# A fused attention and FP4 feed-forward block: the first step of each unit refilled, the next batch's q and k made earlier, the context scaled and added in one VectorE pass

## Chip, cores and metric

The kernel runs on one core of one Trainium2 chip. The metric is the device time of one launch in microseconds (us). The kernel before takes 4181.91 us, the median of three runs (4179.44 to 4182.91).

## What is computed

The input is x of shape (8, 1024, 512) in float32: 8 batches of 1024 rows.

```
q, k, v = split of (x @ w_qkv) into 3 x 16 heads of 32
scores  = q k^T / sqrt(512)          per head, 1024 x 1024
ctx     = softmax(scores) @ v
x  = layernorm(x + ctx)
g, y = fp4(x) @ fp4(w_gate)^T, fp4(x) @ fp4(w_up)^T       512 -> 1408
x  = layernorm(x + fp4(silu(g) * y) @ fp4(w_down)^T)      1408 -> 512
```

fp4() rounds each block of 16 values to the grid 0, 0.5, 1, 1.5, 2, 3, 4, 6 times the block's own scale.

## The kernel before, in words

After a stage that prepares the weights (some 235 us), a loop runs over the 8 batches. The last quarter of each batch's attention also starts on the next batch: it turns its x and makes its first q and k.

**Attention.** The 16 heads are 4 groups of 4. A unit is one group and one half of the query rows, so a batch has 8 units (`UNITS`), numbered 0 to 7, and a unit has 8 steps (t = 0 to 7), one for each tile of 128 keys. In a step TensorE (PE) makes the scores of 4 heads (`scores`, into the three PSUM banks SC), ScalarE (ACT) takes their exponentials (`exponentials`), and PE multiplies the values by the probabilities of the step before (`weigh`, float32, into the bank CT). GpSimd (POOL) adds up the probabilities of seven of the steps (`sum_probs`).

The softmax needs a row maximum before its exponentials. So 32 further score products per unit are made one unit ahead: PE writes each to a bank of the ring R, and VectorE (DVE) reduces it (`maximum`, jobs `("max", u + 1, n)`). At step 7 PE turns the 16 negated maxima (job `neg`, line 668), DVE splits them into two bf16 parts (`maxima_transposed`, lines 585 and 586), and two DMAs of SyncE (SP) put them below the queries as two more rows (`stack_maxima`, line 521). The first score of the next unit waits for them (`m_loaded`).

**The ring R** has four PSUM banks (`RING = 4`), handed out in the order of the jobs. A job of PE waits in `take` until the job that had its bank before has been read. A projection (`proj`, q, k or v of a group, in four quarters of 0.65 us spread over steps) holds one bank from its first quarter until its low part is made, so the others mostly turn over three banks.

**The end of a unit.** In unit u + 1 PE makes the sums over keys (job `sum`, step 1), turns them (`sumT`, step 2; DVE: `reciprocals`), and turns the context of unit u, four transposes into one bank (`ctx`, step 3, `CTX_STEP`, line 685). DVE's `context_out` multiplies it by the reciprocals in one instruction of 128x512 (line 1282) into `ctx_new`; POOL's `add` (line 1072) then adds `ctx_new` to x.

**Order of work.** `unit_jobs(u, t)` deals the jobs of a step to six places; PE runs a score after places 0, 1, 3 and 4 (`SCORES_AT`) and `weigh` after place 2 (`VALUES_AT`), but in step 0 of a unit it runs `weigh` of the last step first, ahead of place 0. `MADE` says which projection jobs a unit makes and how many quarters in each step. Each engine runs its part of that order in program order. DVE's comes from `vector_steps`: maxima, `neg`, `sumT` and `ctx` in PE's order, a low part behind the next maximum.

**q and k of a group** are copied from `split` to the stacked operands by 12 DMAs for each of k, q0 and q1 (`stack`, line 515), in SP's queue with the loads of x and `stack_maxima`. The first maximum product in unit 7 is the next batch's, and waits for k and q0 of group 4.

**Feed-forward.** Eight tiles of 128 rows, with gate and up products (line 1509), silu, two quantisations on DVE, transposes (lines 1461 and 1471) and the down product (line 1530). In its first tile DVE runs `context_out` of unit 7, `maxima_transposed`, `first_moments(2)` and then the first `quantise_h`, one after another.

## Time and profile before

| | |
|---|---|
| median of 3 runs | 4181.91 us |
| the profiled execution | 4181.16 us, its span 4179.5 us |
| PE busy | 3839.0 us, 92% |
| DVE busy | 3069.8 us, 73% |
| POOL busy | 2279.9 us, 55% |
| ACT busy | 1753.3 us, 42% |
| mean granted TensorE clock | 0.971 of full speed |

The profile is one execution, with all times counted from its start. Between the first and the last batch it repeats every 494 us or so: some 285 us of attention and 210 us of feed-forward. All stretches below are from the fifth batch, which begins near 2203 us, unless a line says otherwise. An engine's busy share does not say whether it waits at the place that matters; the waits and the order of single instructions do. In a timeline a row's duration ends when its result is written, and a next instruction can start before that; the spacing of starts is what a queue of instructions takes.

### The profile page before, as it was taken

Reading aid. Unit: us, or ns where it says so; the run is one execution under the profiler, and the core shown is the slowest. Engines: PE = TensorE matmul, PEld = TensorE weight load, DVE = VectorE, ACT = ScalarE, POOL = GpSimd, SP = SyncE. Lnnn points to the kernel's source line nnn. Section 1 sums busy time; section 2 is a strip of 40 time slices with the busy share of each in tenths; the row PEclk is TensorE's granted clock in tenths of the full one; section 3 lists DMA queues with packets and bytes.
Section 4 is the critical chain, followed back from the end, with each engine's and each line's share of the span. In section 5 each row is a group of like instructions: output and inputs, shape, how many; then the busy total and the mean of one; then the engine's idle time right before and its main releaser. Section 6 shows DMA issues by size and latency. Waiting matters only on the chain. (4 is left out here: it accounts for less than half of the span.)

```text
span 4179.5 us, 61806 instructions
## 1 busy us (share of the span) xinstructions
PE 3839.0 (92%) x22985; PEld 1713.9 (41%) x22985; DVE 3069.8 (73%) x4929; ACT 1753.3 (42%) x3104; POOL 2279.9 (55%) x1446
## 2 busy tenths in 40 slices
PE   3489999999999999999999999999999999999999
PEld 2234344333543345433453335433354334533345
DVE  8866687666866678666786668766686667866777
ACT  3345522554235532455225552255323553245522
POOL 4368622885248832687227862388424873268722
PEclk8689999999999999999999999999999999999999
DMA  5110010111010110111101101101101011010110
GB/s 164 40 59 26 26 49 31 26 31 51 22 34 21 38 43 23 29 31 31 46 18 40 28 21 54 32 21 31 51 23 32 25 34 47 18 36 24 31 49 21
DMA packets 106559, 152.56 MB, mean 37 GB/s; under 512 B 28176, under 2 KB 55568, under 8 KB 106128
## 3 DMA queue, kind: packets, MB, share of 16 engines
q1 hardware_dynamic: 106256, 148.49, 11.5%
q8 instruction: 194, 3.18, 0.3%
q14 instruction: 109, 0.89, 0.1%
HBM read 76.28 MB, written 19.66 MB: 23 GB/s over the span
## 5 line engine op out<-in xcount | busy, mean ns | idle before, releaser
L571 DVE TENSOR_REDUCE mx<-R 128x1 f32<-128x512 f32 x2080 | 1355.6, 686 | 633.4 <-PE R L663 624.0
L1186 ACT ACTIVATE arena<-SC 128x512 f32<-128x512 f32 x1344 | 750.2, 600 | 425.8 <-PE SC L1438 425.6
L1509 PE MATMUL SC<-wgu,split 128*128 128x512 f16 (+1 forms) x3456 | 724.4, 364 | 0.6
L1084 POOL TENSOR_TENSOR wd<-wd,arena 128x1024 f32<-128x1024 f32 x208 | 484.7, 2356 | 39.8 <-ACT arena L1186 39.8
L663 PE MATMUL R<-ks_even,qs_even 96*128 96x512 bf16 x1056 | 418.9, 404 | 88.7 <-issue 44.5
L1110 POOL TENSOR_TENSOR arena<-arena,sc_h 128x704 f32<-128x704 bf16 (+2 forms) x136 | 176.1, 1312 | 576.7 <-DVE arena L496 576.7
L1186 ACT ACTIVATE wd<-SC 128x512 f32<-128x512 f32 x704 | 402.5, 601 | 191.5 <-PE SC L1438 184.7
L1509 PEld LDWEIGHTS SC<-wgu,split 128*128 128x128 f16 x3456 | 338.7, 98 | 344.2 <-issue 13.1
L1227 ACT ACTIVATE arena<-SC,gain 128x512 f32<-128x512 f32 (+1 forms) x192 | 125.1, 651 | 775.1 <-PE R L1509 390.8
L643 PE MATMUL R<-xT,wqkv 128*128 128x512 bf16 x1632 | 433.7, 389 | 4.3 <-issue 4.0
L663 PE MATMUL R<-arena 96*128 96x512 bf16 x1024 | 384.9, 382 | 9.3 <-DVE xT L558 8.1
L1438 PE MATMUL SC<-qs_even,ks_even 98*128 98x512 bf16 x1024 | 367.8, 387 | 4.9 <-ACT arena L1186 4.2
L1438 PE MATMUL SC<-arena 98*128 98x512 bf16 x1024 | 364.5, 385 | 4.7 <-ACT wd L1186 2.1
L663 PEld LDWEIGHTS R<-ks_even,qs_even 96*128 96x128 bf16 x1056 | 106.2, 101 | 374.4 <-DVE mx L571 184.7
L1084 POOL TENSOR_TENSOR spill<-spill,arena 128x1024 f32<-128x1024 f32 x104 | 245.5, 2361 | 6.1 <-ACT arena L1186 5.2
L1084 POOL TENSOR_TENSOR x<-x,arena 128x1024 f32<-128x1024 f32 x104 | 245.1, 2357 | 0.7
L643 PEld LDWEIGHTS R<-xT,wqkv 128*128 128x128 bf16 x1632 | 162.2, 100 | 202.7 <-issue 22.8
L1509 PE MATMUL R<-wgu,split 128*128 128x512 f16 (+1 forms) x1152 | 243.9, 361 | 0.0
L1100 POOL TENSOR_TENSOR split<-spill,sc_x 128x512 f32<-128x512 bf16 x64 | 67.6, 1057 | 319.1 <-DVE spill L496 319.1
L1530 PE MATMUL CT<-wd,arena 128*128 128x512 bf16 x1056 | 234.4, 379 | 0.0
L1530 PE MATMUL R<-wd,arena 128*128 128x512 bf16 x1056 | 234.4, 379 | 0.0
L653 PEld LDWEIGHTS R<-wqkv,xT 128*128 128x128 bf16 x3168 | 200.8, 99 | 58.5 <-issue 10.5
(139 smaller groups left out, 5692.9 us busy)
## 6 DMA issues: line engine op xcount, KB each, us to landing
x<-n_L_attn_embeddings_dram SPq DMA_DIRECT2D x136, 256.0 KB, 2.8
wd<-wd_kept SPq DMA_DIRECT2D x32, 512.0 KB, 5.8
out_dram<-x SPq DMA_DIRECT2D x64, 256.0 KB, 2.0
ks_even<-split SPq DMA_DIRECT2D x204, 64.0 KB, 2.0
qs_even<-split SPq DMA_DIRECT2D x408, 32.0 KB, 1.8
arena<-split SPq DMA_DIRECT2D x192, 64.0 KB, 2.0
arena<-split SPq DMA_DIRECT2D x384, 32.0 KB, 1.8
wd<-wd_kept SPq DMA_DIRECT2D x16, 384.0 KB, 7.5
```

Of the source, the lines that this page charges most:

```text
L571: nc.vector.reduce_max(mx[:, j:j + 1], ring_of(ring, job)[:, :], AX_X).then_inc(max_done, 1)
L643: last = nc.tensor.matmul(ring_of(ring, job)[:, :], wqkv[:, part_w, k, c:c + P], xT[:, part_x, k, half * BANK:(half + 1) * BANK], start=(k ...
L653: last = nc.tensor.matmul(ring_of(ring, job)[:, tt * P:(tt + 1) * P], xT[:, part_x, k, t * P:(t + 1) * P], wqkv[:, part_w, k, c:c + P], st ...
L663: last = nc.tensor.matmul(ring_of(ring, job)[:, :], qs[g % 2][0:STACK, a % 2, hl, t * P:(t + 1) * P], ks[g % 2][0:STACK, hl, half * BANK:( ...
L1084: nc.gpsimd.tensor_tensor(acc[u % 2][i], first, probs_of(s)[:, hs, :], ALU.add).then_inc(pool_sum, 1)
L1100: nc.gpsimd.tensor_tensor(blocks_of(q_x), blocks_of(r_x), spread(sc_x[:, :], H // BLK), ALU.mult).then_inc(qx_done, 1)
L1110: nc.gpsimd.tensor_tensor(blocks_of(q_h[:, cols]), blocks_of(r_h[:, cols]), spread(sc_h[:, c], c.stop - c.start), ALU.mult).then_inc(qh_do ...
L1186: nc.scalar.activation(probs_of(s)[:, hd, :], SC[e % SLOTS][:, :], ACT.Exp, scale=SCALE).then_inc(exp_done, 1)
L1227: nc.scalar.activation(sg[:, k % 2, 0:CHUNKS[c][1]], GU[k % 2][0][:, 0:CHUNKS[c][1]], ACT.Silu, scale=un_gain).then_inc(silu_done, 1)
L1438: nc.tensor.matmul(SC[e % SLOTS][:, :], ks[g % 2][0:STACK_M, hd, t * P:(t + 1) * P], qs[g % 2][0:STACK_M, u % 2, hd, :], start=True, stop= ...
L1509: last = nc.tensor.matmul(GU[kk % 2][which][:, 0:w], xhT[i % 2][:, part_x * KH + k, :], wgu[:, part_w * KH + k, which * I + first:which * ...
L1530: last = nc.tensor.matmul(Y[i % 2], hT[i % 2][:, 2 * TILE_K * c + part_h * tiles + n, :], wd[:, part_w * KI + k, :], start=(k == 0 and m = ...
```

## The change

- **Step 0 of a unit.** Place 0 (two maximum products and a quarter) now runs ahead of `weigh` of the last step, and ScalarE copies the context (`context`) after its own jobs of place 0. Maximum 2 moves to place 1, maximum 4 to place 5. In step 1 the job `sum` runs ahead of a maximum product in its place and no longer behind it.
- **q and k of the next batch.** Job 0 of group 4 moves from unit 6 to unit 5 (four quarters in steps 5, 6 and 7), jobs 1, 2 and 3 are made in unit 6 (two quarters in each of steps 1 to 6), and unit 7 keeps job 4 alone.
- **The context.** `context_out` becomes 16 `scalar_tensor_tensor` instructions of 128x32 (four tiles by four heads). Each reads its part of the ring's bank, multiplies it by one column of `rec` and adds x in place. POOL's `add`, the semaphore `added` and the use of `ctx_new` for it are gone.

```diff
--- before.py
+++ after.py
@@ -89,11 +89,10 @@
 BEFORE_FFN = sum(MAX_STEPS_LAST)
 MADE = (((1, (4, 5)), (1, 1, 1, 1, 1, 1, 1, 1)), ((2, (0, 1)), (1, 1, 1, 1, 1, 1, 1, 1)),
         ((2, (2, 3, 4)), (2, 2, 2, 1, 1, 1, 2, 1)), ((2, (5,)), (3, (0, 1)), (2, 1, 1, 2, 1, 2, 2, 1)),
-        ((3, (2, 3, 4)), (2, 2, 2, 1, 1, 1, 2, 1)), ((3, (5,)), (4, 0, 0, 0, 0, 0, 0, 0)),
-        ((4, (0, 1, 2)), (0, 3, 3, 2, 2, 2, 0, 0)), ((4, (3, 4)), (2, 2, 1, 1, 1, 1, 0, 0)))
+        ((3, (2, 3, 4)), (2, 2, 2, 1, 1, 1, 2, 1)), ((3, (5,)), (4, (0,)), (4, 0, 0, 0, 0, 1, 1, 2)),
+        ((4, (1, 2, 3)), (0, 2, 2, 2, 2, 2, 2, 0)), ((4, (4,)), (1, 1, 0, 1, 1, 0, 0, 0)))
 SCORES_AT, VALUES_AT = (0, 1, 3, 4), 2
 SUM_STEP, SUM_T_STEP, CTX_STEP = 1, 2, 3
-ADD_TILE, ADD_TILE_LAST = 3, 2
 LN_MOMENTS, LN_SCALE = 5, 6
 X_TURNS = [(UNITS - 3, t) for t in range(1, TILES)] + [(UNITS - 2, 0)]
 
@@ -125,7 +124,9 @@
         other += [("xT", X_TURNS.index((u, t)), 0)]
     neg = [("neg", u + 1, 0)] if t == TILES - 1 and not ends else []
     if t == 0:
-        return m[0:1] + q[0:1] + m[1:2], [], m[2:3], m[3:4] + q[1:2], other + m[4:5], q[2:] + m[5:]
+        return m[0:1] + q[0:1] + m[1:2], m[2:3], [], m[3:4] + q[1:2], other, m[4:5] + q[2:] + m[5:]
+    if t == SUM_STEP:
+        return [], m[0:1] + q[0:1], m[1:2], other + m[2:3], m[3:4] + q[1:2], m[4:5] + q[2:] + m[5:]
     return [], m[0:1] + q[0:1], m[1:2], neg + m[2:3] + other, m[3:4] + q[1:2], m[4:5] + q[2:] + m[5:]
 
 
@@ -401,7 +402,6 @@
         wd_saved = sem("wd_saved")
         wd_loaded = [sem(f"wd_loaded{c}") for c in range(len(CHUNKS))]
         ctx_done = sem("ctx_done")
-        added = sem("added")
         chain = sem("chain")
         pool_chain = sem("pool_chain")
         var_done = sem("var_done")
@@ -1065,12 +1065,6 @@
                     nc.gpsimd.memset(ks[1][STACK:STACK_M, :, :], 1.0).then_inc(ones_done, 1)
                     pool.wait_ge(ones_done, 1)
 
-                    def add(u):
-                        pool.wait_ge(ctx_done, u + 1)
-                        rows, g = slice(u % 2 * UNIT_TILES, (u % 2 + 1) * UNIT_TILES), u // 2
-                        xa = x[:, rows, g * P:(g + 1) * P]
-                        nc.gpsimd.tensor_tensor(xa, xa, ctx_new[:, :, :], ALU.add).then_inc(added, 1)
-
                     def sum_probs(u, t, i):
                         s, hs = TILES * u + t, slice(2 * i, 2 * i + 2)
                         pool.wait_ge(exp_done, GROUP * s + 2 * i + 2)
@@ -1116,15 +1110,11 @@
                                 inverse_deviation("x", 0)
                             for i in range(2):
                                 sum_probs(u, t, i)
-                            if t == (ADD_TILE if u < UNITS - 1 else ADD_TILE_LAST) and u >= 1:
-                                add(u - 1)
                     scale_x(0)
                     inverse_deviation("x", 1)
                     for i in range(TILES):
                         if i + 1 < TILES:
                             scale_x(i + 1)
-                        if i == 0:
-                            add(UNITS - 1)
                         if 2 <= i < TILES - 1:
                             inverse_deviation("out", i - 2)
                         if i + 2 < TILES:
@@ -1187,8 +1177,6 @@
                                              scale=SCALE).then_inc(exp_done, 1)
 
                     for s, (u, t) in enumerate(steps):
-                        if t == 0 and u >= 1:
-                            context(u - 1)
                         if (u, t) == (UNITS - 1, LN_SCALE):
                             first_norm(0)
                         for n, place in enumerate(unit_jobs(u, t)):
@@ -1199,6 +1187,8 @@
                                     sums(g)
                                 elif kind == "xT":
                                     x_transposed(g)
+                            if n == 0 and t == 0 and u >= 1:
+                                context(u - 1)
                             if n in SCORES_AT:
                                 exponentials(s, SCORES_AT.index(n))
 
@@ -1274,16 +1264,16 @@
 
                     def context_out(u):
 
-                        job = ("ctx", u, 0)
+                        job, g = ("ctx", u, 0), u // 2
                         dve.wait_ge(ring_full, ring.full(job))
                         dve.wait_ge(rec_done, u + 1)
-                        if u >= 1:
-                            dve.wait_ge(added, u)
-                        nc.vector.tensor_tensor(
-                            ctx_new[:, :, :].rearrange("p t (h d) -> p t h d", h=GROUP),
-                            ring_of(ring, job)[:, :].rearrange("p (t h d) -> p t h d", h=GROUP, d=HD),
-                            rec[:, :, :].unsqueeze(3).to_broadcast([P, UNIT_TILES, GROUP, HD]),
-                            ALU.mult).then_inc(ctx_done, 1)
+                        for i in range(UNIT_TILES):
+                            for hd in range(GROUP):
+                                part = x[:, u % 2 * UNIT_TILES + i, g * P + hd * HD:g * P + (hd + 1) * HD]
+                                last = nc.vector.scalar_tensor_tensor(
+                                    part, ring_of(ring, job)[:, i * P + hd * HD:i * P + (hd + 1) * HD],
+                                    rec[:, i, hd:hd + 1], part, ALU.mult, ALU.add)
+                        last.then_inc(ctx_done, 1)
 
                     def moments(name, i, src, free):
 
@@ -1303,7 +1293,7 @@
 
                     for (u, t), jobs in zip(steps, vector_steps(steps)):
                         if (u, t) == (UNITS - 1, LN_MOMENTS):
-                            dve.wait_ge(added, UNITS - 1)
+                            dve.wait_ge(ctx_done, UNITS - 1)
                             first_moments(0)
                         for kind, a, j in jobs:
                             if kind == "proj3":
@@ -1390,7 +1380,7 @@
                             low_h(i - 1, 2)
                         if i + 2 < TILES:
                             if i == 2:
-                                dve.wait_ge(added, UNITS)
+                                dve.wait_ge(ctx_done, UNITS)
                             first_moments(i + 2)
                         dve.wait_ge(h_done, len(CHUNKS) * (i + 1))
                         quantise_h(i, slice(0, I))
@@ -1483,14 +1473,12 @@
 
                     for s, (u, t) in enumerate(steps):
                         places = unit_jobs(u, t)
-                        if t == 0 and u >= 1:
-                            weigh(s - 1)
                         for n, place in enumerate(places):
                             run(place)
+                            if n == (0 if t == 0 else VALUES_AT) and s > 0:
+                                weigh(s - 1)
                             if n in SCORES_AT:
                                 scores(u, t, SCORES_AT.index(n))
-                            if n == VALUES_AT and t > 0:
-                                weigh(s - 1)
                     weigh(len(steps) - 1)
```

## Rows read from the trace of the kernel before

**Rows 1.** Waits of TensorE from 2200 to 2700 us: us, times, longest.
```profile
PE CT L1451 <- ACT arena L1186: 5.1, 5, 1.2
```

**Rows 2.** Timeline of TensorE at the start of unit 2: start, us, instruction, idle before.
```profile
2269.03 0.28 PE L668 MATMUL R<-identf,neg 128*16 128x128 f32 x1
...
2270.70 1.07 PE L1451 MATMUL CT<-wd,v_even 128*32 128x512 f32 x8 [0.96 <-ACT wd L1186]
...
2272.80 0.59 PE L1438 MATMUL SC<-arena 98*128 98x512 bf16 x2
```

**Rows 3.** SyncE's two DMAs of the maxima there, and their time to landing.
```profile
2270.03 1.14 SPq L521 DMA_DIRECT2D arena<-negT  x2
...
DMA to landing us min/median/max: 1.6/1.7/2.0
```

**Rows 4.** Timeline of TensorE around the context's transposes, units 3 and 4.
```profile
2322.59 0.60 PE L685 MATMUL R<-identf,wd 128*128 128x128 f32 x4
...
2324.77 0.38 PE L663 MATMUL R<-ks_even,qs_even 96*128 96x512 bf16 x1
...
2358.65 0.60 PE L685 MATMUL R<-identf,wd 128*128 128x128 f32 x4
...
2360.20 0.39 PE L663 MATMUL R<-ks_even,qs_even 96*128 96x512 bf16 x1
```

**Rows 5.** Timeline of VectorE around the same context, unit 4.
```profile
2359.46 0.68 DVE L1282 TENSOR_TENSOR ctx_new<-R,rec 128x512 f32<-128x512 f32 x1
2360.05 1.88 DVE L571 TENSOR_REDUCE mx<-R 128x1 f32<-128x512 f32 x3
```

**Rows 6.** VectorE groups by shape: busy us, mean ns.
```profile
L1336 DVE TENSOR_TENSOR arena<-R,arena 128x512 bf16<-128x512 f32 x128 | 85.4, 673 | 0.0
...
L1336 DVE TENSOR_TENSOR arena<-R,arena 128x384 bf16<-128x384 f32 x64 | 35.1, 548 | 10.2 <-ACT arena L1219 10.2
```

**Rows 7.** Timeline of VectorE in the feed-forward stage.
```profile
2549.39 0.74 DVE L1354 SCALAR_TENSOR_TENSOR arena<-R,gain,arena 128x512 f32<-128x512 f32 x1
2550.05 0.68 DVE L1336 TENSOR_TENSOR arena<-R,arena 128x512 bf16<-128x512 f32 x1
...
2552.09 0.18 DVE L1294 BATCH_NORM_AGGREGATE mv<-stats 128x2 f32<-128x6 f32 x1
2552.19 0.66 DVE L1336 TENSOR_TENSOR arena<-R,arena 128x512 bf16<-128x512 f32 x1
```

**Rows 8.** Timeline of TensorE at the start of unit 7.
```profile
2445.55 0.28 PE L668 MATMUL R<-identf,neg 128*16 128x128 f32 x1
...
2451.56 0.38 PE L663 MATMUL R<-ks_even,qs_even 96*128 96x512 bf16 x1 [3.27 <-DMA qs_even<-split]
...
2452.86 1.06 PE L1438 MATMUL SC<-arena 98*128 98x512 bf16 x2
```

**Rows 9.** SyncE's queue in units 6 and 7.
```profile
2433.46 8.50 SPq L515 DMA_DIRECT2D ks_even<-split  x12
2442.65 7.48 SPq L515 DMA_DIRECT2D qs_even<-split  x12
2450.17 1.22 SPq L521 DMA_DIRECT2D arena<-negT  x2
```

**Rows 10.** TensorE at the end of unit 5, then VectorE's last low x.
```profile
2410.81 1.07 PE L1451 MATMUL CT<-arena,v_even 128*32 128x512 f32 x8 [1.23 <-ACT arena L1186]
...
2415.23 0.68 DVE L558 TENSOR_TENSOR xT<-R,xT 128x512 bf16<-128x512 f32 x1
```

**Rows 11.** TensorE at the start of the feed-forward stage.
```profile
2523.59 0.63 PE L1471 MATMUL R<-identf,arena 128*128 128x128 f32 x4 [2.20 <-POOL arena L1110]
2524.05 3.79 PE L1509 MATMUL SC<-wgu,split 128*128 128x384 f16 x12
```

**Rows 12.** That place in two of eight batches: busy by engine, granted clock, DMA.
```profile
2029.50:2035.50 6.00, 4.96 (x32) 3.21 (x32) 5.73 (x11) 1.77 (x3) 2.10 (x2) 1.00 0.17 64
2523.00:2529.00 6.00, 5.41 (x26) 3.18 (x27) 5.69 (x11) 1.19 (x2) 2.10 (x3) 0.72 0.24 92
```

## Prediction

> **What bounds the kernel now.** TensorE is busy for 92% of the span and no other engine for over 73%, so I read its waits first, then the single steps around each edit. The view of its waits names one that comes back at the unit starts: five times a batch (three more stand under the other buffer) PE waits for ScalarE's last exponential [rows 1]. In the timeline this is the 0.96 us of idle time before `weigh`; the next unit's first score then starts at 2272.80, 3.77 us after the transposes of the maxima at 2269.03 [rows 2]. Elsewhere in a unit PE's matmuls start without a gap. So the kernel is bound by PE and the order of its queue, and an edit counts by whether PE stands still for more or less. DVE is close behind it where the context is read: its maxima there run back to back [rows 5].
>
> **Step 0 refilled.** Two maximum products and a quarter, some 1.08 us, now lie in the gap ahead of `weigh`. By itself this would give back the whole gap of about 1.1 us. But the first score also waits for two DMAs of the maxima. They are issued from 2270.03, 1.14 us for both; the second, at about 2270.60, lands 1.7 us later, at 2272.30 [rows 3]. That is 3.27 us after the transposes, and the old first score stood at 3.77 us. With 0.06 us from landing to start it can come at 3.34 us: the gain is 0.43 us, and what was a wait for an exponential becomes a wait for this DMA. Six units (1 to 6) give 2.6 us a batch. In unit 6 extra quarters fill the gap before the transposes too; see below.
>
> **q and k earlier.** In unit 7 PE waits 3.27 us for q0 of the next batch, and its first score comes at 2452.86, 7.31 us after the transposes at 2445.55. The two scores there take 1.06 us where the same two took 0.59 us in unit 2: PE then runs at its lower clock [rows 2, 8]. SP issues q0's 12 DMAs from 2442.65 to 2450.13, and the maxima's two are queued behind them, from 2450.17 [rows 9]. In the new order q0's job ends in step 4 of unit 6 and no longer in step 5, with fewer quarters ahead of it, some 5.4 us earlier (a step there lasts 4.1 to 5.5 us between its first scores in the timeline, and two fewer quarters, 1.3 us, run before it). k's ends a step earlier too and has left the queue by then. So q0's DMAs end near 2444.7, land 1.4 us later, and PE asks for them at 2446.1: just in time. The maxima's DMAs then find the queue free, and the first score comes 3.34 us after the transposes: 7.31 − 3.34 = 3.97 us, and 1.6 us more for eight matmuls of the stretch that no longer take twice their 0.22 us. Together 5.6 us.
>
> The moved quarters are of 0.65 us each (four, 2.6 us, go to unit 5 and leave unit 7). In unit 5, where PE waits 1.23 us before `weigh` and for ScalarE earlier in that step [rows 10], some 1.5 us of them is hidden. In unit 7 three of the four save their time; the fourth, in step 5, covered PE while VectorE and GpSimd normalised the first tile, and saves nothing. In unit 6 step 6 hides 0.25 us. But job 1 now comes first in unit 6, and it needs all eight tiles of x: its first quarter, which started at about 2415.0, must wait for the low part that DVE ends at 2415.91 [rows 10], 0.9 us. Sum: 1.95 − 1.1 + 0.25 − 0.9 = +0.2, taken as +0.3 us.
>
> **The context on VectorE.** This is the part that decides. One instruction that kept DVE for 0.59 us (2359.46 to the next start at 2360.05 [rows 5]) becomes 16, and POOL's add, which PE never waited for, goes. The trace has no 128x32 instruction of this kind. The nearest is the `scalar_tensor_tensor` of the feed-forward stage, with one PSUM source and a per-partition scalar: 0.74 us for 512 columns, 0.66 us from start to start [rows 7]. 128 columns less take 125 ns less (673 to 548 ns, another operation [rows 6]), about 1 ns a column; a slope of 1.04 ns, one column a cycle, fits the two best of these. 480 columns less leave 0.66 − 0.50 = 0.16 us from start to start and 0.25 us for the last one. I take 0.165 us. The lower bound is the shortest spacing in the trace, 0.10 us from a two-column instruction to the next; the upper is 0.25 us, no overlap at all.
>
> A rule bears on this choice. The Trainium skill (VectorE: DVE Perf Modes, "The TRN2 errata") gives a VectorE instruction that reads PSUM 120 cycles plus one per column at 0.96 GHz, and advises tiles of at least 512 elements because many small tiles pay the fixed part each. By it, as an estimate, each would take 158 ns and the forecast would be some 7 us lower. It gives 658 ns for a whole bank, and this trace has 660 ns for the form with a scalar but 590 ns for the plain one [rows 5, 7]; by the plain form's fixed part a small one would cost 0.09 us. The rule and the form with the scalar agree, and they speak against the change.
>
> Who waits? DVE starts the context 0.81 us after PE's transposes at 2358.65 [rows 4, 5]. The bank comes free at 0.81 + 15 × 0.165 + 0.25 = 3.54 us, and PE sees it 0.06 us later: 3.60 us. While a projection holds a bank, the three others go to the context and two maxima, and the third maximum product, the first of step 4, takes the context's bank. It started at 2360.20, 1.55 us after the transposes, and in unit 3, with a quarter between, at 2324.77, 2.18 us after them [rows 4]. So PE stands for 2.05 us in units 2, 4 and 7 and for 1.42 us in units 3 and 6. In unit 1 the next projection takes that bank a matmul later (1.85 us); in unit 5 an x transpose lies between, but its low part waits behind the same 16 (1.9 us). Sum: 6.15 + 2.84 + 3.75 = 12.8 us a batch. DVE has the maxima behind it read again within a step, and PE gets none of it back, since it is what bounds.
>
> The context of unit 7 is read in the first feed-forward tile, ahead of the quantisation for which PE already waits 2.20 us [rows 11]; the next instruction started 0.61 us after it and would now start 16 × 0.165 = 2.64 us after it: 2.0 us more. After that wait the granted clock was 0.72 in the stretch in five of eight batches and 1.00 in three [rows 12]; 12 gate matmuls of 384 columns then took 3.79 us [rows 11], against 12 × 0.17 at the full clock, 1.7 us more. A longer wait should bring the low clock in all eight: 3/8 × 1.7 = 0.6 us. The new waits of 2.05 us lie just under the one that does this, and the idle times of 0.96 and 1.23 us are followed by scores at full pace [rows 2, 10]. I count one such fall a batch: 1.7 us.
>
> **Sum.** Gains 2.6 + 5.6 + 0.3 = 8.5 us; losses 12.8 + 2.0 + 0.6 + 1.7 = 17.1 us; net 8.6 us a batch, 69 us for eight. The profiled execution took 4181.16 us (span 4179.5), 0.75 us under the median of the runs: 4181.2 + 69 = 4250 us. A nanosecond per instruction is worth 7 × 15 + 16 = 121 ns a batch, 0.97 us in all.
>
> **Rivals.**
> - *The small instructions are cheap*, the other side. At 0.10 us each the losses fall by 65 × 0.97 = 63 us and the clock term by up to 14 us: 4173 to 4187 us. It decides at about 0.10 us. For it: the short spacing in the normalisation, and the plain form's small fixed part. Against: the form with a scalar. 13%.
> - *PE does not wait for the context's bank*, since the maxima make room in another way. Then 12.8 and 1.7 go, and 5.9 us are gained: 4134 us. Against it: the product in question starts 0.06 us after the context ends [rows 4, 5]. 10%.
> - *No overlap*: each instruction starts when the one before has ended, 0.25 us. 85 × 0.97 = 82 us more: 4332 us. The Trainium skill (same page, "Two Vector instructions with no wait between them") holds an instruction back only where its operands start in other quadrants than the last one's; here all start at partition 0, which speaks against it, and no row shows it. 10%.
> - *The low clock after nearly every context wait*: six falls and not one, 5 × 1.7 = 8.5 us a batch: 4318 us. For it: the wait of 2.20 us does so in five of eight. The Trainium skill (TensorE: Matmul & The Clock Gate, "The HAM clock gate") has activity hold the clock up, so each standstill counts against it. 12%.
> - *q and k do not come early enough*: a DMA or DVE step is late and half of the 5.6 us or all of it stays: 4272 to 4295 us. 10%.
>
> My own case has 45%, and its own range is 4215 to 4285 us. The range to 8 in 10 leaves out the second rival and the far end of the third: 4165 to 4320 us. What a measurement here can tell from no change is 0.2%, 8.4 us. Faster than that holds the second rival and most of the first, 0.20; within it 0.08; slower 0.72.
>
> **What would show it.** Right: 16 instructions on the context's line about 0.165 us apart; PE waits of 1.4 to 2.1 us on it in step 4 of every unit but the first; first scores 3.3 us after the transposes, released by the DMA of the maxima; no wait for q0 in unit 7; a feed-forward wait of about 4.2 us. Wrong: a spacing near 0.10 us, PE waits under 1 us there, or a low clock in most units.

## The result, and the profile after

The changed kernel takes 4255.58 us (median of four runs, 4252.03 to 4264.54) against 4181.99 us for the kernel before on the same chip: a ratio of 1.018, 95% interval 1.0163 to 1.0198. It is slower by 74 us. The profiled execution is the slowest of the four, 4264.54 us with a span of 4262.9 us, so its rows add up to some 9 us more than the median. All stretches are again of the fifth batch, which now lies near 2243 to 2750 us, unless the text says otherwise.

The page's first part and the waits of TensorE over the whole span (us, times, longest):

```profile
PE 3864.9 (91%) x22985; PEld 1725.6 (40%) x22985; DVE 3185.3 (75%) x5889; ACT 1752.5 (41%) x3104; POOL 2201.8 (52%) x1382
```

```profile
PE R L663 <- DVE x L1273: 72.1, 48, 1.8
...
PE R L1461 <- POOL arena L1104: 33.2, 8, 4.2
PE R L1451 <- DVE mx L571: 15.2, 8, 2.0
...
PE R L643 <- DVE x L1273: 12.6, 8, 1.6
PE CT L1441 <- ACT wd L1176: 11.9, 16, 1.0
PE SC L1428 <- DMA qs_even<-negT: 11.2, 24, 0.6
```

The first row is the largest part of the loss. It had no counterpart before: PE's maximum product (line 663) waits for VectorE's write of x (line 1273, the context), 48 times, six in each batch. With the row of line 643 (8 times, a projection quarter of unit 1 that takes the context's bank) it makes 84.7 us, 10.6 us a batch. VectorE's busy time rose by only 115 us, 2.7% of the span, and PE is as busy as ever: no busy share shows this.

**Around the context**, unit 4, TensorE and then VectorE (start, us, instruction, idle before). It answers to [rows 4, 5]:

```profile
2400.52 0.60 PE L685 MATMUL R<-identf,wd 128*128 128x128 f32 x4
...
2401.84 0.38 PE L1428 MATMUL SC<-qs_even,ks_even 98*128 98x512 bf16 x1
...
2404.01 0.39 PE L663 MATMUL R<-ks_even,qs_even 96*128 96x512 bf16 x1 [1.79 <-DVE x L1273]
```

```profile
2401.33 2.62 DVE L1273 SCALAR_TENSOR_TENSOR x<-R,rec,x 128x32 f32<-128x32 f32 x16
2403.86 2.48 DVE L571 TENSOR_REDUCE mx<-R 128x1 f32<-128x512 f32 x4
```

The transposes start at 2400.52, VectorE's 16 instructions 0.81 us later, as before, and they end at 2403.95, 3.43 us after the transposes. PE's product starts 0.06 us after that. It stood 1.55 us after the transposes before and stands 3.49 us after them now: 1.94 us later, in unit 4 as in units 2 and 7. VectorE then runs four maxima back to back: it has a backlog, and PE is the one that pays for it. By shape (busy, mean ns):

```profile
L1273 DVE SCALAR_TENSOR_TENSOR x<-R,rec,x 128x32 f32<-128x32 f32 x1024 | 167.6, 243 | 0.8
```

One takes 243 ns, and 2.62 us for 16 means (2.62 − 0.25) / 15 = 0.158 us from start to start.

**Start of a unit**, unit 2, TensorE, then SyncE; it answers to [rows 2, 3]. The transposes of the maxima start at 2307.66:

```profile
2308.43 0.81 PE L643 MATMUL R<-xT,wqkv 128*128 128x512 bf16 x3
2309.28 0.39 PE L663 MATMUL R<-arena 96*128 96x512 bf16 x1
2309.60 1.06 PE L1441 MATMUL CT<-wd,v_even 128*32 128x512 f32 x8
2310.99 0.39 PE L1428 MATMUL SC<-arena 98*128 98x512 bf16 x1 [0.32 <-DMA arena<-negT]
```

```profile
2308.66 1.14 SPq L521 DMA_DIRECT2D arena<-negT  x2
```

`weigh` no longer waits 0.96 us for the exponential; the first score waits 0.32 us for the DMA instead, and comes 3.33 us after the transposes (it was 3.77).

**Start of unit 7**, TensorE and SyncE's queue, to be read against [rows 8, 9]:

```profile
2496.56 0.38 PE L663 MATMUL R<-ks_even,qs_even 96*128 96x512 bf16 x1
2496.78 0.83 PE L653 MATMUL R<-wqkv,xT 128*128 128x128 bf16 x12
2497.95 1.06 PE L1441 MATMUL CT<-arena 128*32 128x512 f32 x8
2499.35 0.39 PE L1428 MATMUL SC<-arena 98*128 98x512 bf16 x1 [0.34 <-DMA arena<-negT]
```

```profile
2487.14 7.47 SPq L515 DMA_DIRECT2D qs_even<-split  x12
2497.00 1.15 SPq L521 DMA_DIRECT2D arena<-negT  x2
```

The wait of 3.27 us for q0 is gone: q0's issues end 2.4 us ahead of the maxima's, where they used to end just as these began. The first product on group 4 starts without an idle time, and one score takes 0.39 us, the pace of the full clock.

**Entry to the feed-forward stage**, TensorE, against [rows 11]:

```profile
2534.67 0.66 PE L1451 MATMUL R<-identf,split 128*128 128x128 f32 x4 [1.99 <-DVE mx L571]
...
2572.21 1.09 PE L1461 MATMUL R<-identf,arena 128*128 128x128 f32 x4 [4.15 <-POOL arena L1104]
2573.09 4.05 PE L1497 MATMUL SC<-wgu,split 128*128 128x384 f16 x12
```

The wait ahead of the first quantised tile grew from 2.20 to 4.15 us. The wait ahead of the transposes of x (line 1451) is 1.99 us; in the trace of before it is 0.76 us.

**The granted clock.** The stretch of unit 2's context and the one behind it, the same two things in unit 4, and behind unit 7's context (busy by engine, then granted clock, DMA share, GB/s):

```profile
2325.00:2332.00 7.00, 5.21 (x29) 1.89 (x27) 6.14 (x23) 2.84 (x6) 6.94 (x3) 1.00 0.12 33
2332.00:2335.40 3.40, 3.40 (x13) 0.74 (x13) 2.30 (x5) 1.26 (x3) 2.35 (x1) 0.52 0.03 10
2398.00:2405.00 7.00, 5.21 (x30) 2.03 (x29) 6.14 (x22) 2.92 (x6) 6.88 (x4) 1.00 0.13 35
...
2516.30:2520.00 3.70, 3.70 (x23) 1.70 (x23) 2.38 (x4) 1.08 (x2) 2.37 (x2) 0.54 0.00 0
```

After a wait of 1.8 us in unit 2 PE ran 3.4 us at 0.52 of full speed, the 1.2 GHz level, while it was busy all the time; eight matmuls of `weigh` then took 1.89 us instead of 1.06. Such a fall costs some 1.7 us: unit 2 lasts 36.3 us in the two batches without one and 37.9 to 38.2 us in the six with one. Counted over the eight batches in the records of the granted clock, there are six such falls behind unit 2's context, four behind unit 4's, three behind unit 5's and eight behind unit 7's, and none in units 1, 3 and 6: 21, or 2.6 a batch. None of these places fell before. All low stretches behind the weight stage together last 117.5 us before and 174.1 us after.

### The profile page after: what moved, and what is told of

It is laid out like the page before. It is cut to its first block and busy times, and to the rows that moved or that the text cites. A ratio compares the mean times of both kernels' runs of the same rounds, so it can differ in the third digit from the quotient of the medians.

```text
span 4262.9 us, 62702 instructions
## 1 busy us (share of the span) xinstructions
PE 3864.9 (91%) x22985; PEld 1725.6 (40%) x22985; DVE 3185.3 (75%) x5889; ACT 1752.5 (41%) x3104; POOL 2201.8 (52%) x1382
## 5 line engine op out<-in xcount | busy, mean ns | idle before, releaser
L663 PE MATMUL R<-arena 96*128 96x512 bf16 x1024 | 393.9, 386 | 45.5 <-DVE x L1273 34.3
L1085 POOL TENSOR_SCALAR var_eps<-mv 128x1 f32<-128x1 f32 x128 | 28.0, 219 | 424.5 <-DVE mv L1284 423.8
```

The lines of the kernel that those rows point to most:

```text
L663: last = nc.tensor.matmul(ring_of(ring, job)[:, :], qs[g % 2][0:STACK, a % 2, hl, t * P:(t + 1) * P], ks[g % 2][0:STACK, hl, half * BANK:( ...
```

## The experiments

### The parts by themselves

Four kernels on one chip, whose kernel before took 4181.81 us. The first has both order edits with the old context (`ctx_new` and POOL's `add`), the second the context edit alone, the third and the fourth one order edit each.

```diff
 # in e1_order_parts and e3_step0_only
-        return m[0:1] + q[0:1] + m[1:2], [], m[2:3], m[3:4] + q[1:2], other + m[4:5], q[2:] + m[5:]
+        return m[0:1] + q[0:1] + m[1:2], m[2:3], [], m[3:4] + q[1:2], other, m[4:5] + q[2:] + m[5:]
...
 # in e1_order_parts and e4_qk_only
-        ((3, (2, 3, 4)), (2, 2, 2, 1, 1, 1, 2, 1)), ((3, (5,)), (4, 0, 0, 0, 0, 0, 0, 0)),
+        ((3, (2, 3, 4)), (2, 2, 2, 1, 1, 1, 2, 1)), ((3, (5,)), (4, (0,)), (4, 0, 0, 0, 0, 1, 1, 2)),
-        ((4, (0, 1, 2)), (0, 3, 3, 2, 2, 2, 0, 0)), ((4, (3, 4)), (2, 2, 1, 1, 1, 1, 0, 0)))
+        ((4, (1, 2, 3)), (0, 2, 2, 2, 2, 2, 2, 0)), ((4, (4,)), (1, 1, 0, 1, 1, 0, 0, 0)))
...
 # in e2_context_only
-                        nc.vector.tensor_tensor(
...
+                                last = nc.vector.scalar_tensor_tensor(
```

> Both order edits (step 0 refilled, q and k of the next batch earlier), with the context as before: one VectorE instruction of 128x512 and GpSimd's add. Theory (the 16 small instructions hold the ring's bank and TensorE waits for it): in the changed kernel's trace those waits are some 12 us a batch, the feed-forward wait is 2 us longer and three falls of the clock a batch cost some 5 us; without them 4095 to 4115 us, no wait on the context's line, and the granted clock low only at the start of a batch and in the feed-forward stage. Rival (the new orders themselves cost, by later x, k or q): 4182 us or more.

Measured: 4114.51 us, ratio 0.984 (0.9827 to 0.9854).

> The kernel before with the context edit alone. Theory: 12 us of waits a batch in step 4 of units 1 to 7, 2 us in the feed-forward stage and 2 to 5 us of lower clock: 4182 + 8 x 16 to 19 = 4310 to 4335 us. Rival (a wait of 2 us costs only itself and the falls of the clock come from the new order): 4295 us, with no more low clock than before. Rival (GpSimd's freed time pays for it): under 4260 us.

Measured: 4313.36 us, 1.0312 (1.0298 to 1.0326).

> The kernel before with step 0 refilled alone. Theory (the first score of a unit waits for the DMA of the maxima, 3.3 us after their transposes): first scores at 3.3 us where they stood at 3.77 us, 0.43 us in six units: 4161 us. Rival (the refill gives back the whole gap ahead of weigh, 1.1 us in seven units): 4120 us. In unit 7 nothing is gained, since q0 of the next batch comes as late as before.

Measured: 4161.54 us, 0.9952 (0.9938 to 0.9965).

> The kernel before with the earlier q and k alone. Theory: the wait of 3.3 us for q0 in unit 7 and the low clock behind it go (some 5 us), less about 1 us for the wait on the last tile of x in unit 6 and 1 us at the start of the feed-forward stage: 4145 to 4160 us. Rival (the moved quarters only shift a wait, to the x tiles or to the feed-forward start): 4182 us, no change.

Measured: 4149.59 us, 0.9922 (0.9909 to 0.9936).

The order parts give 67.3 us, 8.4 us a batch; the context edit costs 131.5 us alone and 4255.6 − 4114.5 = 141.1 us on top of the order parts. So the change is a gain and twice that gain in loss. The waits name the context edit in its own kernel in the same numbers as in the whole change, and the feed-forward wait of 4.2 us goes with it (e2_context_only, whole span):

```profile
PE R L661 <- DVE x L1271: 72.0, 48, 1.8
...
PE R L1459 <- POOL arena L1102: 33.2, 8, 4.2
```

The two order edits give 20.3 and 32.2 us alone, 14.8 us less than together. In e3_step0_only the row of q0 shows why: the refilled step asks for q0 earlier, and the wait for it grew from 3.27 to 5.5 us.

```profile
PE R L665 <- DMA qs_even<-split: 43.1, 8, 5.5
PE SC L1440 <- DMA qs_even<-negT: 11.6, 24, 0.6
```

### Where the time of the context edit lies, by unit

Mean length of a unit over seven batches, from its first score to the next unit's (unit 7: to the next batch's first score), profiled executions of e1_order_parts and of the changed kernel; the wait is the start-to-start shift of the matmul that waits, a fall is counted at 1.7 us:

| unit | with the old context | after | longer by | wait | falls |
|---|---|---|---|---|---|
| 0 | 29.82 | 30.11 | 0.29 | | |
| 1 | 31.28 | 33.03 | 1.75 | 1.73 | |
| 2 | 34.22 | 37.49 | 3.27 | 1.94 | 6/8: 1.3 |
| 3 | 33.94 | 35.22 | 1.28 | 1.30 | |
| 4 | 34.22 | 36.85 | 2.63 | 1.94 | 4/8: 0.9 |
| 5 | 36.27 | 38.76 | 2.49 | 1.83 | 3/8: 0.6 |
| 6 | 37.82 | 39.08 | 1.26 | 1.30 | |
| 7 and feed-forward | 247.83 | 253.70 | 5.87 | 1.93 | 8/8: 1.7 |

The units sum to 18.8 us a batch, and the two executions differ by 4264.54 − 4114.51 = 150.0 us, 18.8 for each of eight. In units 1 to 6 wait and falls account for the lengthening within 0.2 us. In unit 5 the product that waits stands 1.51 us later and the next one 1.83 us; in the batches without a fall the unit is 1.82 us longer. The last row splits in three. Up to the last score of unit 7 it is 3.1 us: the wait and the fall make 3.6, and 0.4 us of that comes back at the last `weigh`, which waits 0.96 us for its exponential and no longer 1.37 us. The wait at line 1451 is 0.4 us longer, but its transposes come no later behind the last score. The transposes of the quantised tile add 1.9 us, and 0.9 us lies behind them, where the low stretches of the clock are longer.

### Is it PE's cover, or the number of instructions?

Two kernels from the changed one. The first moves one projection quarter into step 3 of units 1, 2, 4 and 7, where it comes between the context's transposes and the product that waits. The second halves the number of instructions: 8 of 128x64, so that every second head is scaled by its neighbour's reciprocal.

```diff
 # c1_quarter_in_step3
-MADE = (((1, (4, 5)), (1, 1, 1, 1, 1, 1, 1, 1)), ((2, (0, 1)), (1, 1, 1, 1, 1, 1, 1, 1)),
-        ((2, (2, 3, 4)), (2, 2, 2, 1, 1, 1, 2, 1)), ((2, (5,)), (3, (0, 1)), (2, 1, 1, 2, 1, 2, 2, 1)),
-        ((3, (2, 3, 4)), (2, 2, 2, 1, 1, 1, 2, 1)), ((3, (5,)), (4, (0,)), (4, 0, 0, 0, 0, 1, 1, 2)),
-        ((4, (1, 2, 3)), (0, 2, 2, 2, 2, 2, 2, 0)), ((4, (4,)), (1, 1, 0, 1, 1, 0, 0, 0)))
+MADE = (((1, (4, 5)), (1, 1, 1, 1, 1, 1, 1, 1)), ((2, (0, 1)), (1, 1, 1, 2, 1, 1, 1, 0)),
+        ((2, (2, 3, 4)), (2, 2, 2, 2, 1, 1, 1, 1)), ((2, (5,)), (3, (0, 1)), (2, 1, 1, 2, 1, 2, 2, 1)),
+        ((3, (2, 3, 4)), (2, 2, 2, 2, 1, 1, 1, 1)), ((3, (5,)), (4, (0,)), (4, 0, 0, 0, 0, 1, 1, 2)),
+        ((4, (1, 2, 3)), (0, 2, 2, 2, 2, 2, 2, 0)), ((4, (4,)), (1, 1, 0, 2, 0, 0, 0, 0)))
```

```diff
 # c2_eight_of_64
-                            for hd in range(GROUP):
-                                part = x[:, u % 2 * UNIT_TILES + i, g * P + hd * HD:g * P + (hd + 1) * HD]
+                            for hd in range(0, GROUP, 2):
+                                part = x[:, u % 2 * UNIT_TILES + i, g * P + hd * HD:g * P + (hd + 2) * HD]
...
-                                    part, ring_of(ring, job)[:, i * P + hd * HD:i * P + (hd + 1) * HD],
+                                    part, ring_of(ring, job)[:, i * P + hd * HD:i * P + (hd + 2) * HD],
```

> The changed kernel with one projection quarter of units 1, 2, 4 and 7 moved into step 3, where TensorE makes it between the context and the product that takes the context's bank. Theory (the low clock comes from the length of the wait: 1.9 us brings it, 1.3 us does not): the waits of units 2, 4 and 7 fall from 1.95 to 1.3 us and that of unit 1 from 1.7 to 1.3 us, 2.3 us a batch, and with them two of the three falls of the clock go, 1.7 us each: 45 us less than the changed kernel, 4210 us. Rival (the falls hang on something else in these units): the waits shrink alone, 4237 us. Rival (the quarters are missed where they were): 4255 us.

Measured: 4233.12 us against 4180.67 for the kernel before on that chip, 1.0119 (1.0103 to 1.0134): 22.5 us under the changed kernel.

> The changed kernel with the context in 8 instructions of 64 columns in place of 16 of 32; two neighbouring heads are scaled by the reciprocal of the first, so the values of every second head are scaled wrongly. Theory (a fixed cost of about 0.125 us for each instruction, plus one cycle a column): 0.19 us apart, the bank free 1.1 us sooner, waits of 0.85 us and 0.25 us, no fall of the clock on them, 4255 - 8 x 14 = 4145 us. Rival (the cost goes by the columns, or by reading and writing x in place): the same waits as in the changed kernel, 4255 us.

Measured: 4163.74 us, 0.9957 (0.9944 to 0.9971): 91.8 us under the changed kernel.

Waits of TensorE in the one and in the other:

```profile
PE R L663 <- DVE x L1273: 65.4, 56, 1.4
```

```profile
PE R L663 <- DVE x L1273: 21.8, 32, 0.8
...
PE R L1461 <- POOL arena L1104: 25.2, 8, 3.2
```

The moved quarter does what it should at its place: no wait on the context's line is over 1.4 us, and falls went from 21 to 8 (none behind unit 7's context, three in unit 2, one in unit 4, four in unit 5). Yet it gives only half of what the theory gave, some 4 us more than its rival (4237 us), and the fewer falls are nearly all of it: 13 × 1.7 = 22 us. In batches without a fall units 2 and 4 last as long as in the changed kernel, 36.3 and 36.2 us in both. VectorE's backlog is as long as before, and PE meets it at the next maxima (0.38 and 0.30 us in units 2 and 4); unit 1 lacks the quarter in step 7 and is 0.15 us longer. Unit 7 with the feed-forward stage keeps its gain, 251.5 us instead of 253.7. So the cover shortens the wait, but apart from the falls of the clock it gives no time back in units 2 and 4.

With half the instructions VectorE starts one each 0.192 us (duration 0.275), the bank is free 2.43 us after the transposes instead of 3.43, the waits, start to start, are 0.93 us in units 2, 4 and 7 and 0.30 us in 3 and 6, and no fall follows any of them. The time is still 19 us over the forecast of 4145 us: units 1 and 5 are also 0.7 and 0.8 us longer than in e1_order_parts, and at the quantised tile the wait is 1.0 us longer. 32 columns more cost 0.034 us, and 0.158 − 0.034 = 0.124 us of each instruction is there whatever its width. Worked up to 512 columns that is 0.124 + 512 × 1.06 ns = 0.67 us, beside 0.66 us in [rows 7]: one line through all three. The fixed parts of 16 instructions make 2 us.

### Is it the bank, or VectorE's time?

If only the bank were held too long, a copy that frees it at once would cure it. Two kernels read the bank with one copy to `ctx_new` and run the 16 instructions from there, in one burst or three behind each following maximum.

```diff
 # c3_copy_then_burst
+                        nc.vector.tensor_copy(ctx_new[:, :, :].rearrange("p t c -> p (t c)"),
+                                              ring_of(ring, job)[:, :]).then_inc(ctx_done, 1)
...
-                                    part, ring_of(ring, job)[:, i * P + hd * HD:i * P + (hd + 1) * HD],
+                                    part, ctx_new[:, i, hd * HD:(hd + 1) * HD],
...
 # c4_copy_then_spread, besides
                                 maximum(a, j)
+                                add_parts(pending[:3])
+                                pending = pending[3:]
```

> The changed kernel, with the context first copied from its bank to SBUF in one instruction of 128x512, which frees the bank; the 16 small instructions then read the copy. Theory A (TensorE waits since VectorE is kept for 2.6 us, whichever bank it holds): the wait moves to the maxima behind it and is no shorter, VectorE is kept 0.5 us longer: 4255 to 4290 us. Theory B (only the context's bank is what holds TensorE up): the waits go, 4255 - 8 x 17 = 4120 us.

Measured: 4657.67 us, 1.1139 (1.1124 to 1.1155).

> The same copy, but the 16 small instructions are laid behind the next six maxima, three at a time, except in the feed-forward stage. Theory A (a burst on VectorE is what costs, not its amount): VectorE falls behind by 0.3 to 0.5 us for each maximum and most of the wait stays away: 4150 to 4190 us. Rival (VectorE's total work counts): as the burst, 4255 us or more.

Measured: 4621.72 us, 1.1052 (1.1037 to 1.1067).

Both missed by some 400 us, and no theory of mine had it. c3_copy_then_burst in the timelines of VectorE and GpSimd, then its line's durations (min/median/max ns), then TensorE's waits:

```profile
2581.41 0.68 DVE L1271 COPY ctx_new<-R 128x512 f32<-128x512 f32 x1
2582.13 8.23 DVE L1282 SCALAR_TENSOR_TENSOR x<-ctx_new,rec,x 128x32 f32<-128x32 f32 x16
```

```profile
2581.25 4.64 POOL L1079 TENSOR_TENSOR wd<-wd 128x1024 f32<-128x1024 f32 x2
2585.86 2.33 POOL L1079 TENSOR_TENSOR wd<-wd,arena 128x1024 f32<-128x1024 f32 x1
```

```profile
L1282 DVE SCALAR_TENSOR_TENSOR x<-ctx_new,rec,x x1024: 235/239/2380, 279.6 to 4469.9; 128x32 f32<-128x32 f32 x171
```

```profile
PE R L664 <- DVE mx L572: 334.0, 63, 7.7
```

The burst takes 8.23 us instead of 2.62. Within it the second, third and fourth instruction start 1.44, 3.74 and 6.04 us after the first, and the rest follow each other at 0.16 us; GpSimd's additions of the probabilities end at 1.47, 3.76 and 6.06 us on the same scale. So the first three small instructions each lasted until a GpSimd instruction of 2.3 us was over. The median one takes 239 ns, as against 243 in the changed kernel, and the first burst after GpSimd has gone quiet, in the feed-forward stage, takes 2.69 us. Spreading them changed the mean from 520 to 553 ns and no more. The form that reads PSUM never showed this, with GpSimd as busy (243 ns in the mean). The Trainium skill (SBUF — State Buffer, "Who interferes with whom") says that a VectorE instruction with two SBUF inputs contends with a GpSimd instruction that reads SBUF, and calls the ports that the two share an exclusive lock. These traces agree: both tensor inputs, `ctx_new` and x, are in SBUF here, and only x is in the changed kernel. So the question of the bank needed another experiment, and whether the same instructions cost less when they are spread stays open.

c5_burst_on_next_bank keeps the old context instruction and POOL's `add` (it is e1_order_parts), and VectorE runs 16 instructions of the same form on the bank of the next maximum, into scratch. VectorE's time is spent, but the context's bank comes free early. In the feed-forward stage, for unit 7's context, it runs none.

```diff
                             elif kind == "max":
+                                if burst:
+                                    small_ones(a, j)
+                                    burst = False
                                 maximum(a, j)
...
+                            nc.vector.scalar_tensor_tensor(
+                                junk[i], ring_of(ring, job)[:, i * HD:(i + 1) * HD],
+                                rec[:, i // 4, i % 4:i % 4 + 1], identf[:, 0:HD], ALU.mult, ALU.add)
```

> Both order edits with the context as before (one VectorE instruction, which frees its bank after 0.7 us, and GpSimd's add), plus 16 instructions of the changed kernel's form and size behind it; they read the bank of the next maximum product and write unused scratch, so they add nothing to the output. Theory A (TensorE waits since VectorE is kept for 2.6 us): the wait moves to the bank of that maximum, two products later, and is as long, 2.0 us or 1.4 us, with falls of the clock: 4114 + 8 x 14 to 17 = 4225 to 4250 us. Theory B (it is the context's bank, held for 2.6 us, that costs): 4114 to 4130 us.

Measured: 4263.0 us against 4180.77, 1.0194 (1.018 to 1.0207). Its waits of TensorE, and one group of its small instructions (busy, mean ns):

```profile
PE R L665 <- DVE mx L573: 82.9, 63, 1.9
```

```profile
L1313 DVE SCALAR_TENSOR_TENSOR amax<-R,rec,identf 128x32 bf16<-128x32 f32 x280 | 49.1, 242 | 0.2
```

The loss is there again, 148 us over e1_order_parts, which has no such row: PE now waits for a maximum where it waited for the context. That the total is so near to the 141 us of the changed kernel is partly chance: there is no longer wait at the quantised tile here, and units 1 and 5 lose more (3.2 and 4.5 us against 1.8 and 2.5). The comparison by unit is the better one: units 2, 3, 4 and 6 are 3.6, 1.4, 2.6 and 1.3 us longer than in e1_order_parts, and in the changed kernel 3.3, 1.3, 2.6 and 1.3 us. The ring turns over three banks, and whatever job VectorE is late with, PE comes round to it within a step. The cause is VectorE's 2.6 us ahead of PE's maxima, not that it is the context's bank which they hold (this kernel keeps the old instruction too, so its piece is some 0.6 us longer). A burst that reads no bank of the ring at all was not measured free of GpSimd.

### What e1_order_parts still leaves

Three kernels from e1_order_parts: the maxima turned two places earlier in step 7; quarters of units 6 and 7 moved (unit 6 waits less for its x); both.

```diff
 # n1_neg_earlier
-    return [], m[0:1] + q[0:1], m[1:2], neg + m[2:3] + other, m[3:4] + q[1:2], m[4:5] + q[2:] + m[5:]
+    return [], neg + m[0:1] + q[0:1], m[1:2], m[2:3] + other, m[3:4] + q[1:2], m[4:5] + q[2:] + m[5:]
 # n2_quarters_moved
-        ((4, (1, 2, 3)), (0, 2, 2, 2, 2, 2, 2, 0)), ((4, (4,)), (1, 1, 0, 1, 1, 0, 0, 0)))
+        ((4, (1, 2, 3)), (0, 0, 4, 2, 2, 2, 2, 0)), ((4, (4,)), (1, 1, 0, 1, 0, 1, 0, 0)))
```

> Both order edits with the context as before, and the transposes of the maxima moved from place 3 to place 1 of step 7, ahead of weigh. Theory (the DMA of the maxima now sets the first score of a unit): the DMA lands 1.2 us sooner, first scores start behind weigh with no wait, 0.6 us in six units: 4114 - 29 = 4085 us. Rival (VectorE's negated maxima are not ready that early, or the first score waits for an exponential anyway): 4114 us.

Measured: 4094.98 us, 0.9795 (0.9781 to 0.9808).

> Both order edits with the context as before, and two quarters moved: unit 6 starts job 1 in step 2 and no longer in step 1 (four quarters in step 2), unit 7 makes a quarter in step 5 and none in step 4. Theory (1.0 us of waiting for the last tile of x in unit 6, 0.7 us at the start of the feed-forward stage): 4114 - 13 = 4101 us. Rival (x low is late for the next product anyway, and the normalisation bounds the start of the feed-forward stage whatever TensorE does before it): 4114 us.

Measured: 4106.48 us, 0.9824 (0.981 to 0.9837).

> The last two together. Theory: 4114 - 42 = 4072 us. If either is refuted alone, what the other gives.

Measured: 4085.01 us (4082.23 to 4086.72), 0.9769 (0.9756 to 0.9782).

Each gives about two thirds of what was expected. In n2_quarters_moved unit 6 is 1.45 us shorter, but the wait at the feed-forward entry, from which 0.7 us was to come, is as long as in e1_order_parts. In n1_neg_earlier the first score no longer waits for its DMAs, and the transposes of the maxima wait for VectorE instead (one such wait of 1.1 us is in e1_order_parts too):

```profile
PE R L670 <- DVE neg L577: 8.2, 17, 1.1
```

This is the version to keep: 96 us under the kernel before and 171 us under the changed one.

## Why the prediction was right, and where it was off

It said 4250 us and it came to 4255.6. Step by step:

- **Step 0 refilled, 0.43 us a unit.** The first score comes 3.33 us after the transposes (3.34 forecast), held by the maxima's DMA. Alone the edit is worth 20.3 us, 2.5 a batch, against 2.6. The agreement is partly luck: units 1 to 4 are each 0.64 to 0.68 us shorter in e1_order_parts than before (31.28 beside 31.96 in unit 1). 0.43 us of it is the earlier first score, and 0.23 us comes in step 1, where `sum` now runs directly behind `weigh`, and for which the prediction had no term. Alone, the edit gives part of that back to the longer wait for q0: units 6 and 7 together are 1.1 us longer.
- **q0 just in time, 5.6 us.** Its wait is gone, the maxima's DMAs find the queue free and the low clock at unit 7's start is gone, as forecast. The first scores of units 3 and 6 come later than 3.34 us: in unit 3 (3.43 to 3.71 us) PE waits for the maxima's DMA, in unit 6 (3.87 us) it does not wait at all, since its own matmuls run up to the score.
- **The moved quarters, +0.3 us.** The wait for the last low part of x in unit 6 is 1.03 us (0.9 forecast). What the quarters gave in unit 7 was too high. The wait at the feed-forward entry was 0.76 us, and it is 1.5 us with the q and k edit alone (waits of TensorE over the whole span, of the kernel before and of e4_qk_only, below); with the last `weigh`, whose wait went from 1.10 to 1.4 us, some 1.0 us of the 2.6 us comes back, where 0.65 us was forecast. Nor was it the quarter of step 5 that covered this wait: n2_quarters_moved has one in step 5 again and none in step 4, and the wait is the same (the last of the rows below). The three order terms sum to 8.5 us forecast and 8.4 measured; only the sum was measured, as the edits give 2.5 and 4.0 us a batch alone and 1.9 us more together.

```profile
PE R L1461 <- POOL split L1100: 6.1, 8, 0.8
```

```profile
PE R L1461 <- DVE mx L571: 12.2, 8, 1.5
```

```profile
PE R L1463 <- DVE mx L573: 12.2, 8, 1.5
```

- **The spacing of a small instruction, 0.165 us.** Measured 0.158. The two ends of the range, 0.10 and 0.25 us, were both far; the form with a scalar was the right row and the plain form was not.
- **Who waits, 12.8 us.** Start to start the waits are 1.73, 1.94, 1.30, 1.94, 1.83, 1.30 and 1.93 us, 12.0 in all, in the units forecast and each 0.07 to 0.12 us shorter (1.85, 2.05, 1.42, 2.05, 1.9, 1.42, 2.05), which is what 15 spacings of 0.158 and not 0.165 us make.
- **The feed-forward wait, 2.0 us.** 4.15 us against 2.20, forecast 4.2.
- **The clock, 1.7 us for one fall a batch.** This is the mis-sized term: 2.6 falls a batch behind the context's waits, 4.5 us. "Just under the one that does this" was too kind to waits of 1.8 us of idle time in a stretch where PE is otherwise busy; they brought the low clock in 21 of the 32 places of units 2, 4, 5 and 7, and never in 1, 3 and 6. The rival with six falls was further off. The low stretches at the feed-forward entry and the batch's end rose as well, from 77 to 103 us over the eight batches; 0.9 us a batch lies behind the quantised tile, where 0.6 us was forecast. So the losses are 12.0 + 2.0 + 4.5 + 0.9 = 19.4 us by their terms, of which 0.4 us comes back at the last `weigh` of unit 7, beside 18.8 us in the profiled executions and 17.6 us by the medians; forecast were 17.1.

So the number was near for the right reason in the main: the wait for the bank, its places and its size are as forecast. The clock term was too small by 2.8 us a batch, and part of the agreement is luck, since waits that were 0.8 us shorter, and errors inside the order terms, made up for some of it.

## What to carry to other kernels

A fused pass that turns one wide instruction into many narrow ones pays the fixed part of each: here 0.124 us times 16, against one GpSimd addition that nobody waited for. On an engine that feeds a ring of buffers such a burst is not hidden by freeing its own buffer sooner, because the jobs queued behind it are late all the same; cost it by the time that it keeps the engine. Whether the same instructions cost less when spread is not shown here. And split a change into its parts: this one held a version 1.6% faster than the kernel it was meant to improve.

## What the chip showed that I had not expected

- VectorE's 128x32 instruction with both tensor inputs in SBUF takes 239 ns in the median and up to 2380 ns, when it lasts to the end of GpSimd's running addition; 16 of them took 8.23 us instead of 2.62.
- Waits of 1.8 us, each in a stretch where PE is busy for 5.2 of 7.0 us and runs at full clock, were followed by 3.4 us at 1.2 GHz in six of eight batches in unit 2 and in four of eight in unit 4, though the two stretches have the same busy time, 5.21 us. What decides between them stays open. The length of the wait alone does not decide it: in the changed kernel the waits of 1.3 us in units 3 and 6 were never followed by one, nor was the 1.73 us of unit 1, but in c1_quarter_in_step3, where no wait on the context's line is over 1.4 us, eight were. In e2_context_only the same wait in unit 6 was followed by a fall in seven of eight batches.
